# A transformer block and a two-way selective state-space block on one core: the skip term and eight states' forcing by TensorE transposes, and a fifth buffer of states

## The reference, cut to what matters

```
def _ssm(h, in_w, xproj_w, dt_bias, A_log, Dskip, out_w):
    xs, z = jnp.split(h @ in_w, 2, axis=-1)
    xs = jax.nn.silu(xs)
    proj = xs @ xproj_w
    dt = jax.nn.softplus(proj[..., :D_INNER] + dt_bias)
    Bm = proj[..., D_INNER:D_INNER + D_STATE]
    Cm = proj[..., D_INNER + D_STATE:]
    A = -jnp.exp(A_log)
    def step(hst, ins):
        dt_t, B_t, C_t, x_t = ins
        dA = jnp.exp(dt_t[:, :, None] * A)
        hst = hst * dA + (dt_t * x_t)[:, :, None] * B_t[:, None, :]
        y_t = jnp.einsum('bds,bs->bd', hst, C_t)
        return (hst, y_t)
    ...
    y = jnp.swapaxes(ys, 0, 1) + xs * Dskip
    return y * jax.nn.silu(z) @ out_w
```

## Time and profile before

| what | value |
|---|---|
| median of 3 runs | 3308.7 us (3304.81 to 3312.47) |
| the profiled execution's own time | 3316.36 us |
| its span, first to last instruction | 3314.5 us |
| mean granted TensorE clock over the span | 0.97 of full speed |
| busy PE / DVE / ACT / POOL | 3058.3 / 2884.0 / 2904.8 / 2911.3 us |

### The profile page before, as it was taken

The page is one execution under the profiler, slowest core; times in us unless marked ns, Lnnn a source line. Parts: engine busy times, 40 slices in busy tenths (PEclk is TensorE's granted clock), DMA queues, the critical chain, the costliest instruction groups (busy, mean ns, idle before and its releaser), DMA issues.

```text
span 3314.5 us, 71769 instructions
## 1 busy us (share of the span) xinstructions
PE 3058.3 (92%) x23032; PEld 2760.6 (83%) x23032; DVE 2884.0 (87%) x3203; ACT 2904.8 (88%) x6357; POOL 2911.3 (88%) x1552
## 2 busy tenths in 40 slices
PE   8778999999999999999999999999999999998877
PEld 6568988898888988889888898888888898887766
DVE  2269999899989998899998999899988999989985
ACT  1189999898989989899998999899898989989993
POOL 0069999998999999999998999999999999999995
PEclk6699999999999999999999999999999999999998
DMA  5011111111111111111111111112111111111210
GB/s 179 0 42 45 45 46 54 43 52 44 46 51 45 52 44 47 51 50 44 46 54 44 51 45 45 53 45 52 44 47 50 51 46 45 45 50 44 55 47 26
DMA packets 163039, 162.61 MB, mean 49 GB/s; under 512 B 17610, under 2 KB 156874, under 8 KB 162644
## 3 DMA queue, kind: packets, MB, share of 16 engines
q1 hardware_dynamic: 162644, 157.69, 17.5%
HBM read 154.44 MB, written 3.18 MB: 48 GB/s over the span
## 4 chain that ended last, share of the span: by engine, by line
PE 50%; ACT 23%; issue 11%; DVE 8%; POOL 7%; DVEq 0%; ACTq 0%; POOLq 0%; DMA 0%; SPq 0%
PE ps L1263 13%; ACT dA L584 12%; PE ps L1247 12%; ACT uBT L570 6%; PE ps L1010 6%; POOL hst L417 5%; DVE hst L909 5%; PE ps L1245 4%; PE ps L1082 3%; PE ps L1019 3%; PE ps L1057 3%; PE ps L1066 1%; PE ps L1255 1%; PE ps L1131 1%; POOL uBT L430 1%
## 5 line engine op out<-in xcount | busy, mean ns | idle before, releaser
L417 POOL TENSOR_TENSOR hst<-hst,C_sb 128x1024 f32<-128x1024 f32 x1024 | 2447.3, 2407 | 176.1 <-DVE hst L909 172.7
L909 DVE TENSOR_TENSOR_SCAN hst<-dA,ps 128x512 f32<-128x512 f32 x2048 | 2376.7, 1203 | 146.3 <-PE ps L1263 112.9
L584 ACT ACTIVATE dA<-dt,A 128x255 f32<-128x255 f32 x4096 | 1745.0, 501 | 1.4 <-DVE hst L909 1.2
L1263 PE MATMUL ps<-ident,hst 128*128 128x128 f32 x8192 | 1240.7, 274 | 46.8 <-POOL hst L417 46.7
L1247 PE MATMUL ps<-ident,uBT 128*128 128x128 f32 x7104 | 1084.5, 275 | 52.6 <-DVE hst L909 39.8
L570 ACT ACTIVATE uBT<-uT,BT 128x512 f32<-128x512 f32 x1376 | 936.4, 717 | 117.3 <-PE ps L1247 89.2
L1263 PEld LDWEIGHTS ps<-ident,hst 128*128 128x128 f32 x8192 | 963.2, 141 | 62.9 <-POOL hst L417 62.2
L1247 PEld LDWEIGHTS ps<-ident,uBT 128*128 128x128 f32 x7104 | 844.6, 142 | 195.3 <-DVE hst L909 69.4
L430 POOL TENSOR_TENSOR uBT<-uT,BT 128x512 f32<-128x512 f32 x400 | 427.2, 1068 | 1.4 <-PE ps L1245 1.4
L1245 PE MATMUL ps<-uBT,uT 128*128 128x128 f32 x2176 | 302.7, 284 | 33.9 <-DVE hst L909 27.9
L1245 PEld LDWEIGHTS ps<-uBT,uT 128*128 128x128 f32 x2176 | 272.9, 197 | 45.7 <-DVE hst L909 35.9
(11 more groups left out here) (146 smaller groups left out, 2176.0 us busy)
## 6 DMA issues: line engine op xcount, KB each, us to landing
C_sb<-c_dram SPq DMA_DIRECT2D x1024, 128.0 KB, 2.9
gate_l<-gate_rows_dram SPq DMA_DIRECT2D x16, 256.0 KB, 3.8
x_att<-in_x_dram SPq DMA_DIRECT2D x8, 256.0 KB, 3.6
w<-in_L_cond_W_dram SPq DMA_DIRECT2D x2, 1024.0 KB
out_dram<-x_glu SPq DMA_DIRECT2D x8, 256.0 KB, 3.1
wg<-in_L_cond_mlp_w_dram SPq DMA_DIRECT2D x3, 512.0 KB, 11.0
w_xp<-_L_cond_fwd_xproj_w_dram SPq DMA_DIRECT2D x1, 1280.0 KB, 12.5
w_xp<-_L_cond_bwd_xproj_w_dram SPq DMA_DIRECT2D x1, 1280.0 KB, 14.4
```

The source lines that it names most:

```text
L417: pool.tensor_tensor(h, h, C_sb[:, n % FED:n % FED + 1, :].to_broadcast([P, KI, NB]), ALU.mult).then_inc(hC_ready.sem, 1)
L584: done = act.activation(dA[:, n % NT, c, lo:hi], dt[:, d, c, lo:hi], ACT.Exp, scale=A[:, d, c, n:n + 1])
L909: dve.tensor_tensor_scan(pair(hst[:, n % NR]), pair(dA[:, n % NT]), ps[:, BANK_U + (2 * n + e) % (2 * NU), :][:, way], 0.0, ALU.mult, ALU. ...
L1263: last = pe.matmul(ps[:, BANK_Y + j, c * P:(c + 1) * P], hst[:, n % NR, c, j * P:(j + 1) * P], ident[:, :], start=False, stop=(n == NS - 1 ...
```

## The change

The skip term is no longer a product with a diagonal. VectorE multiplies `xsT` in place by D, one instruction of 1024 columns, in step `dts` 23 of each of the 16 preparations, and `start_y` only transposes it. The eight scalings that made `skip_diag` go, and so does the tensor itself. The memory of `skip_diag` (4096 bytes for each partition) is what a fifth buffer of states takes (NR = 5). Since 64 is no multiple of 5, the first four states of a pass still reuse the buffer of the state four back, and state 4 that of nine back; `reuse` says so. The states 1, 3, 61 and 63 leave `BY_DIAGONAL` in both directions, so that they are forced like any other odd state; 22 to 27 (forward) and 55, 57 and 59 (backward) stay.

```
-    NR = 4
+    NR = 5
+    reuse = lambda n: NR if n >= NR else NS % NR + (NR if n >= NS % NR else 0)
     BEHIND = 3
-    BY_DIAGONAL = ((1, 3, 22, 23, 24, 25, 26, 27, 61, 63), (1, 3, 55, 57, 59, 61, 63))
+    BY_DIAGONAL = ((22, 23, 24, 25, 26, 27), (55, 57, 59))
...
-        skip_diag = sb("skip_diag", [P, 2, KI, P])
...
+        skip_ready = flow("skip_ready")
...
-                for d in range(2):
-                    for c in range(KI):
-                        dve.tensor_scalar(skip_diag[:, d, c, :], ident[:, :], D_col[:, d, c:c + 1], None, ALU.mult).then_inc(skip_ready, 1)
...
                     if i == 22:
                         dve.wait_ge(uT_mm.sem, uT_mm.at(p, 1))
                         dve.tensor_copy(uT[:, d], ps[:, BANK_P:BANK_P + 2, :].rearrange("p a n -> p (a n)")).then_inc(uT_ready.sem, 1)
+                    if i == 23:
+                        dve.tensor_tensor(xsT[:, :, :], xsT[:, :, :], D_col[:, d, :].unsqueeze(2).to_broadcast([P, KI, NB]),
+                                          ALU.mult).then_inc(skip_ready.sem, 1)
                     yield
...
-                    dve.wait_ge(y_mm.sem, y_mm.at(r, e + 1 - 2 * NR))
+                    dve.wait_ge(y_mm.sem, y_mm.at(r, e + 1 - 2 * reuse(n)))
...
-            def start_y(p, d):
+            def start_y(p):
+                pe.wait_ge(skip_ready.sem, skip_ready.at(p, 1))
                 pe.wait_ge(g_ready.sem, g_ready.at(p, 0))
                 for j in range(TT):
                     for c in range(KI):
-                        pe.matmul(ps[:, BANK_Y + j, c * P:(c + 1) * P], xsT[:, c, j * P:(j + 1) * P], skip_diag[:, d, c, :],
-                                  start=(c == 0), stop=False, skip_group_check=True)
+                        pe.matmul(ps[:, BANK_Y + j, c * P:(c + 1) * P], xsT[:, c, j * P:(j + 1) * P], ident[:, :],
+                                  start=(c == 0), stop=False, is_transpose=True, skip_group_check=True)
...
-            pe.wait_ge(skip_ready, 2 * KI)
```

More of the change, by code:

```diff
@@ L253, in cond_transformer_mamba_kernel @@
         dve_setup, rows_ready, mods_ready, bn_turns = map(sem, ("dve_setup", "rows_ready", "mods_ready", "bn_turns"))
-        att_mm, att_mods, wqk_ready, skip_ready = map(sem, ("att_mm", "att_mods", "wqk_ready", "skip_ready"))
+        att_mm, att_mods, wqk_ready = map(sem, ("att_mm", "att_mods", "wqk_ready"))
         offset_turns, hT_turns = sem("offset_turns"), sem("hT_turns")
@@ L1274, in state @@
                     if n == BEHIND and e == 0:
-                        start_y(p, d)
+                        start_y(p)
                     if n >= BEHIND:
```

## The result

The changed kernel takes 3339.9 us (median of 4 runs, 3337.1 to 3341.6) against 3308.0 us (3304.8 to 3312.5): a ratio of 1.0095, 95% interval [1.0083, 1.0107], 32 us slower. I had said 3299 us with a range of 3282 to 3315. The profiled executions differ by 25.1 us in span (3339.6 - 3314.5). Before's lies 8 us above its median and after's 1.5 us, so 7 us of the 32 have no place in the two traces.

A forecast was written before the change was run, and what follows sets the result against it. No engine simply bounds it: four are busy 87 to 92% and take turns being late. 1.6 + 11.2 + 5.5 - 2.4 - 3.5 - 3.7 + 1.4 = 10.1 us won, so 3299 us, range 3282 to 3315.

The forecast's parts named there:

- The fifth buffer elsewhere: Away from the turns: scans start up to 0.44 us earlier; 0.1 for each of 14 passes, 1.4 us won.
- the lock: SBUF port shared by VectorE and GpSimd, taken in turn: the new multiply costs VectorE 1.1 to 3.5 us, taken as 2.2.
- The forward-to-backward turns: Seven turns from a forward to a backward pass, 1.6 us won at each, 11.2 us in all.
- Both terms of it: At each forward-to-backward turn: 1.0 us from the shorter start_y, 0.6 from TensorE's cheaper forcing of the four states.
- rival D: At the turns, transposes replace matmuls and TensorE's clock falls: 46 us slower, 3355 us; chance 0.03.
- the clock's dip at the turns: Sign against the prediction: TensorE's clock dips longer at the turns; it was expected to stay at 1.00.
- The multiply in backward passes: After state 59's first half, where VectorE has no idle time: the skip multiply's 2.2 us count in full.
- In forward middles: After state 27 of seven forward passes: TensorE's 1.1 us slack covers part of the multiply; 0.5 lost each, 3.5 us.
- The jumps: Five turns with a jump back: 2.3 us idle and 1.0 of start_y won, 2.2 lost; 1.1 each, 5.5 us.
- The tail and the start: Tail, where GpSimd never idles: 3.7 us lost to dearer forcings and one multiply. Start: 1.6 us won without eight scalings.
- Rival A: GpSimd's lock makes each multiply cost 3.5 us: 3321 us, chance 0.14; it decides from about 2.9 us a multiply.

The follow-up runs named there:

- e3: The changed kernel with four buffers of states instead of five (NR = 4, reuse always 4): 3327.8 us, ratio 1.0058 to the kernel before.
- e5: The changed kernel, five buffers, but scans of states 40 to 53 of backward passes wait as with four: 3328.7 us, ratio 1.0055.
- e7: The changed kernel with the first half of state 4's forcing transposed five times over, ahead of start_y: 3322.0 us, ratio 1.0040.
- e9: The changed kernel with multiply on ScalarE, state 4's first half-forcing transposed five times, and backward states 40 to 53 waiting as with four buffers: 3291.9 us.
- e6: The changed kernel with the skip multiply on ScalarE, as four instructions in the same step: 3316.8 us, ratio 1.0024.
- e2: The kernel before with the skip change alone (multiply on VectorE, start_y by transposes; four buffers, old BY_DIAGONAL): 3317.4 us, ratio 1.0028.
- e4: The changed kernel with the old BY_DIAGONAL (states 1, 3, 61, 63 by diagonal again): 3334.0 us, ratio 1.0073.
- e8: The kernel before with the skip term by transposes and its multiply on ScalarE; four buffers, old diagonals: 3291.9 us, ratio 0.9941.

## Why the prediction was wrong

*The fifth buffer elsewhere* is the step that failed first. "Only the step into the next stage can gain", with bounds of 0 and 6.2 us, left out a loss. A gain was there: 0.6 us a backward pass, 4.5 in all, inside the bounds (the states 6 to 52 show 1.0 a pass, but e3, with four buffers, has 0.35 of it too). But scans that start about half a microsecond earlier take GpSimd's product with them, past an instruction of VectorE that waits for ScalarE. It cost 2.4 us in each of seven passes, 16.6 us. e5 shows it. I priced the lock for the new instruction and not for those whose order against GpSimd the change would turn.

*The forward-to-backward turns* failed as badly: 11.2 us to be won, 2.0 lost. Both terms of it were real, as e7 and e9 show (-2.1 a turn). The step that failed is the one from TensorE's saved time to the turn's time, with the clock left at full speed. The gate doesn't come as much sooner as TensorE does: against the start of the pass TensorE was done 2.6 us sooner and the gate came 0.8 sooner. So the work saved ahead of it turned into a pause, and the clock fell behind the pause, at a price of 1.6 us for each 3.4 us at 0.50. I had weighed the clock, as rival D, but for the wrong cause, transposes in place of matmuls; e7, with yet more transposes, has full clock. The prediction had named the clock's dip at the turns as what would make it wrong, and it did. The Trainium skill (TensorE: Matmul & The Clock Gate, Why this matters for your kernels) warns of pauses between TensorE's bursts inside a kernel. The traces agree in the main (0.50 behind 2.80 us, 1.00 behind e7's 1.05), though not at every turn (e6), and that was the rule to weigh.

*The multiply in backward passes*: forecast 2.2, measured 2.35 us, and 1.9 where it began later in GpSimd's product (e2, e4). *In forward middles*: the instruction was the cheap one (1.2 us), but I took its cover from TensorE's slack where VectorE itself was full; 1.1 instead of 0.5 each, 4.5 us in all.

*The jumps*: forecast 3.3 us won against 2.2 lost; measured 2.4 against 2.3. With the multiply gone from VectorE (e6, e8) the 2.3 aren't won: VectorE waits for them behind the jump. So at these five turns the multiply costs nothing, and the saving of the change isn't paid out. What VectorE waits for there is open; the packets of instructions beside e8 are a hint and no proof.

*The tail and the start* were right to about 1 us; for the start that is luck in part, as the first scan scatters by 5 us. *Rival A* (the lock dearer) had the right direction, though 3321 us is still 19 short, and for no right reason: the multiplies' mean is 1.84 us, not over 2.9.

What stays open besides: what decides whether the clock falls behind a pause of 2.8 us, and the 7 us by which the medians differ more than the two profiles. The fifth buffer on the kernel before alone was not tried: its memory is that of `skip_diag`.

## What to carry to other kernels

Work taken off an engine ahead of a wait is not yet time won: look whether the wait's other side comes sooner too, and if not, what the pause does to the clock. Before a change that lets an engine start earlier, list the instructions that share a port with what it starts, and see which of them begin by a margin smaller than the shift; their order, not their length, is what will change. A multiply by a scalar for each partition was hidden on ScalarE, in a kernel where VectorE and GpSimd are both full; try it there.

## What the runs showed of the hardware

- A VectorE instruction with two inputs in SBUF took 1.53 us where it began 0.39 us ahead of GpSimd's product and 3.38 us where it began 0.07 us behind. An added wait that restores the first order (e5) made the kernel 11 us faster.
- Sixteen needless transposes a pass (e7) made the kernel 18 us faster, by keeping TensorE's pause at 1.05 instead of 2.80 us. With a pause of 2.8 us the granted clock behind it was 0.50 in some passes and 1.00 in others of the same program (e6); the scans behind it took the same time as with the short pause where it stayed at 1.00, and 1.6 us more for each 3.4 us at 0.50.
- Behind the loop's jump from pass 5 to 6 VectorE's first pause was 1.59 us, 3.52 us or 5.40 us (before, e6, e8) after the same ten scans of 11.20 us. Seven packets of the instruction queues moved in the 5.40 us.
